# Four column groups for the router logits, and the first mixer chunk moved in between the input turnings

## What is computed

```python
xn = _layernorm(x)
s = _L0_attn_ref(xn, ...)              # the mixer
g = _silu(_L0_ffn_ref(xn, ...))        # mixture of experts, top 1 of 4
x = x + s * g

def _L0_attn_ref(x, ...):
    xn = _rmsnorm(x, rms_w, EPS)
    out_gate = silu(xn @ Wga_w.T) * (xn @ Wgb_w.T)
    f = sigmoid(xn @ Wf_w.T + Wf_b)
    z = (xn @ Wz_w.T) * sigmoid(xn @ Wzg_w.T)
    h = _linear_scan(f, z)             # h[t] = f[t] * h[t-1] + z[t], bfloat16
    return (out_gate * h) @ Wout_w.T + Wout_b + x

def _L0_ffn_ref(x, Wr, br, Wg, Wu, Wd):
    logits = x @ Wr + br               # 4 experts
    top_w, top_idx = top_k(softmax(logits), 1)
    y = (silu(x @ Wg[top_idx]) * (x @ Wu[top_idx])) @ Wd[top_idx]
    return y * top_w
```

## Time and profile before

| | us |
|---|---|
| median of three runs | 1424.99 |
| the profiled execution, its own time | 1422.44 |
| its span, first to last instruction | 1420.6 |
| TensorE busy | 1351.7 (95%) |
| VectorE, ScalarE, GpSimd busy | 1011.4, 880.1, 898.4 |
| mean granted TensorE clock | 0.998 |

### The profile page before, as it was taken

How to read it: one execution, slowest core, us unless ns; L and a number is a source line. 1 busy time by engine, 2 the same in 40 slices (tenths; PEclk the granted TensorE clock), 3 DMA queues, 4 the chain that set the end, 5 groups by cost and what they waited for, 6 DMA issues and landing times.

```text
span 1420.6 us, 24044 instructions
## 1 busy us (share of the span) xinstructions
PE 1351.7 (95%) x8924; PEld 1080.0 (76%) x8924; DVE 1011.4 (71%) x1358; ACT 880.1 (62%) x1459; POOL 898.4 (63%) x570
## 2 busy tenths in 40 slices
PE   7999999999999999998899999999999999999998
PEld 4444559999999988957677777777778678678787
DVE  7755543332232343498998998998989989989897
ACT  3211121111111132488999989999999999999983
POOL 3222211222222212379999998999999999989995
PEclk9999999999999999999999999999999999999999
DMA  9921126766676665331331531523423513513522
GB/s 301 396 97 59 56 84 224 260 260 247 250 268 255 248 226 187 130 88 46 98 93 34 132 92 56 131 68 79 116 75 76 129 50 91 133 46 88 137 68 67
DMA packets 57380, 196.82 MB, mean 139 GB/s; under 512 B 6831, under 2 KB 33583, under 8 KB 49462
## 3 DMA queue, kind: packets, MB, share of 16 engines
q1 hardware_dynamic: 43126, 146.55, 29.3%
q0 software_dynamic: 14144, 48.80, 14.7%
HBM read 141.78 MB, written 31.00 MB: 122 GB/s over the span
## 4 chain that ended last, share of the span: by engine, by line
PE 64%; POOL 17%; ACT 7%; DVE 6%; issue 4%; DMA 1%; SPq 0%; POOLq 0%; DVEq 0%; ACTq 0%
PE bank L1656 17%; POOL hst L733 13%; PE bank L1601 9%; PE bank L1669 9%; PE bank L1830 7%; PE bank L1850 4%; PE bank L1710 4%; ACT dA L940 3%; ACT dbuT L929 3%; DVE hst L1499 3%; PE bank L1702 2%; PE bank L1838 2%; PE bank L1721 2%; PE bank L1740 2%; POOL xpad L676 2%
## 5 line engine op out<-in xcount | busy, mean ns | idle before, releaser
L1499 DVE TENSOR_TENSOR_SCAN hst<-dA,carry,bank 128x512 f32<-128x512 f32 x512 | 632.1, 1269 | 57.3 <-PE bank L1830 37.3
L733 POOL TENSOR_TENSOR hst<-hst,c_bc 128x2048 f32<-128x2048 f32 x127 | 581.8, 4614 | 15.8 <-POOL carry L728 1.8
L940 ACT ACTIVATE dA<-delta,negA 128x512 f32<-128x512 f32 x512 | 353.6, 712 | 7.9 <-DVE hst L1499 7.7
L1830 PEld LDWEIGHTS bank<-ident,dbuT 128*128 128x128 f32 x2048 | 240.1, 141 | 138.5 <-issue 66.4
L1830 PE MATMUL bank<-ident,dbuT 128*128 128x128 f32 x2048 | 311.1, 276 | 32.6 <-DVE hst L1499 28.6
L929 ACT ACTIVATE dbuT<-duT,bT 128x512 f32<-128x512 f32 x382 | 269.0, 711 | 4.9 <-PE bank L1830 4.9
L1656 PEld LDWEIGHTS bank<-f_sb,w_gu 128*128 128x128 f32 x2240 | 256.0, 192 | 4.7 <-issue 2.1
L1656 PE MATMUL bank<-f_sb,w_gu 128*128 128x128 f32 x2240 | 256.9, 275 | 0.7 <-ACT f_sb L797 0.7
L1850 PE MATMUL bank<-ident,hst 128*128 128x128 f32 x1648 | 227.6, 273 | 2.7 <-POOL hst L733 2.4
L661 POOL TENSOR_TENSOR x_sb<-x_sb,neg_half 128x1 f32<-128x1 f32 x35 | 22.6, 647 | 271.4 <-DVE x_sb L1283 271.4
L1850 PEld LDWEIGHTS bank<-ident,hst 128*128 128x128 f32 x1648 | 188.9, 141 | 4.4 <-POOL hst L733 3.9
(11 more groups left out here) (221 smaller groups left out, 1670.1 us busy)
## 6 DMA issues: line engine op xcount, KB each, us to landing
w_gu<-in_w_gu SPq DMA_DIRECT2D x35, 2048.0 KB, 7.5
c_bc<-c_rows SPq DMA_DIRECT2D x64, 512.0 KB, 3.9
hst<-hst POOLq DMA_DIRECT2D x23, 1024.0 KB, 9.0
sorted_x<-sg_a SPq DMA_DIRECT2D x12, 387.0 KB, 11.3
x_sb<-sorted_x SPq DMA_DIRECT2D x35, 129.0 KB, 7.3
x_sb<-in_x SPq DMA_DIRECT2D x8, 512.0 KB, 7.8
w_d<-in_w_d SPq DMA_DIRECT2D x1, 4096.0 KB, 20.3
x_mix<-x_sb SPq DMA_DIRECT2D x1, 4096.0 KB, 30.4
```

The lines of the kernel that those rows point to most:

```text
L733: pool.tensor_tensor(h[:], h[:], c, ALU.mult).then_inc(hc_ready, 1)
L940: act.activation(dA[:, at % DA_BUFS, :], delta[q % B][:, d, :], ACT.Exp, scale=negA[:, d, n:n + 1]).then_inc(dA_ready, 1)
L1499: v.tensor_tensor_scan(h[:, d, :], dA[:, at % DA_BUFS, :], bank[4 + u % 2][:], carry1[q % B][:, n, d:d + 1], ALU.mult, ALU.add).then_inc(s ...
L1830: ins = pe.transpose(bank[4 + u % 2][:, i * P:(i + 1) * P], dbuT[(DS * q + n) % DBU_BUFS][:, i, d * P:(d + 1) * P], ident[:])
```

## The change

1. **Logits.** `w_r` is padded to 32 columns (`QUAD`). Tile i of a chunk is multiplied into partitions 32i to 32i+31 of bank 6, so four matmuls of 128 columns use four column groups of the array. It is done for two chunks at once (16 matmuls for a pair), copied once for the pair, and one matmul with the identity as moving operand (16 columns) brings a chunk's logits to rows.
2. **Order on TensorE.** The turnings use banks 0 and 1 alone. The projections F, ZG, Z, GA and GB of chunk 0, first half, stand between turnings and logits. `ranks` stands in chunk 1.
3. **`w0` on GpSimd.** The scaling moves from ScalarE to GpSimd (`scale_w0`), behind the second of the four `rr0` steps and ahead of the third.
4. **Order on VectorE.** The biases' split, choosing, ranking and placing are spread over chunks 0 and 1: choosing behind the sum of chunk 0, ranking between the halves of chunk 1, placing behind the sum of chunk 1. The rows of chunk 1 get a second buffer (`xn_st_1`, in the second `w_gu` buffer) and a second index tile, and the scatters of chunks 0 and 1 are released together once placing is done. `rows(2)` waits for both chunks' scatters, `rows(3)` for those of chunk 2.
5. **SyncE** stores the mixed rows of chunks 0 and 1 first, then loads `w_gu` for slot 0, waits for the scatters of chunks 0 and 1, then loads slot 1.
6. `mix_st`, `tri`, `ones`, `empty` and `wo_r` move to other buffers.

```diff
-GAP = 152
+GAP = 96
+QUAD = 32
...
-        w_r = sb(l0, "w_r", [P, KB, NE])
+        w_r = sb(l0, "w_r", [P, KB, QUAD])
...
-        mix_st = rt[:].rearrange("p k t e -> p (k t e)").rearrange("p (t d) -> p t d", d=D)
-        tri, ones = (z_sb[:].bitcast(F32)[:, s, 0:P] for s in range(SB))
-        empty = sg_a[:].rearrange("p s c -> p (s c)")[:, 0:FILL * WIDE].rearrange("p (t d) -> p t d", d=WIDE)
+        mix_st = xr_st[:]
+        tri, ones = (w_gu[1][:, 0, 1, s * P:(s + 1) * P] for s in range(SB))
+        empty = w_gu[1][:, 0, 0, 0:FILL * WIDE].rearrange("p (t d) -> p t d", d=WIDE)
...
+        xn_st_1 = w_gu[1][:, 1].rearrange("p k f -> p (k f)")[:, 0:TPC * WIDE].rearrange("p (t d) -> p t d", d=WIDE)
+        logitsT = rt[:, 0:TPC].rearrange("p k t e -> p k (t e)")
+
+        wo_r = w_gu[0][:, 0, 0, 0:SB * D].rearrange("p (s d) -> p s d", s=SB)
         xgT = f_sb[:].bitcast(F32).rearrange("p s c -> p (s c)")[:, 0:KB * P].rearrange("p (k t) -> p k t", k=KB)
...
+            store_mixed(0)
+            store_mixed(1)
             sp.wait_ge(eid_ready, 1)
+            sp.wait_ge(split_ready, 1)
+            sp.wait_ge(zero_filled, 16 * (ROWS // FILL))
             load_up(0)
+            sp.wait_ge(scattered, 2 * 16 * TPC)
             load_up(1)
-            with sp.Fori(0, CHUNKS - 1) as c:
+            with sp.Fori(2, CHUNKS - 1) as c:
                 store_mixed(c)
...
+            def scale_w0():
+                pool.wait_ge(ld_w0, 32)
+                pool.wait_ge(ld_small, 16 * 4)
+                for k in range(KB):
+                    pool.tensor_scalar(w0[:, :, k, :], w0[:, :, k, :], cols0[:, k, 0:1], 1.0, ALU.mult,
+                                       ALU.mult).then_inc(w0_scaled, 1)
+
...
+                if k == 1:
+                    scale_w0()
...
+            def scatter_rows(c, idx, rows):
...
+            scatter_rows(0, idx4, xn_st)
+            scatter_rows(1, idx4_1, xn_st_1)
+            with pool.Fori(2, CHUNKS) as c:
+                scatter_rows(c, idx4, xn_st)
...
+            for c in range(0, CHUNKS, 2):
+                turn_inputs(c)
+                turn_inputs(c + 1)
+                if c == 2:
+                    forget(0, 0)
+                copy_logits(c // 2)
+                if c == 2:
+                    gate_z(0, 0)
+                if c == 4:
+                    gate_a(0, 0)
+            mixer_half(0, 1)
+            mixer_half(1, 0)
             act.wait_ge(shifted, 1)
...
+            mixer_half(0, 0, 0, lambda: split_biases(0))
+            split_biases(1)
+            place_biases()
+            take_logits()
+            mixer_half(0, 1, 0)
+            v.wait_ge(xr_turned, KB * CHUNKS)
+            then(rows(0))
+            add_mix(0)
+            choose()
+            mixer_half(1, 0, 0)
+            rank_rows()
+            mixer_half(1, 1, 0)
+            v.wait_ge(zero_filled, 16 * (ROWS // FILL))
+            then(rows(1, xn_st_1))
+            add_mix(1, xn_st_1)
+            place_rows()
+            tags(0)
+            tags(1, xn_st_1, idx4_1)
+            mixer_half(2, 0, 0)
+            mixer_half(2, 1, 0)
+            then(rows(2))
+            tags(2)
+            add_mix(2)
+            assert [STORED[k] % B for k in range(3)] == [0, 0, 0] and 3 < A_CHUNKS
+
+            def mixer(c, b):
+                rows(c)
+                tags(c)
+                mixer_half(c, 0, b)
+                mixer_half(c, 1, b)
+                add_mix(c)
...
+                    wait_past(pe, xrT_ready, KB * (c - 1) + k + 1)
...
+            def logits(p):
+                pe.wait_ge(xrT_ready, KB * (2 * p + 2))
+                wait_past(pe, logits_copied, p)
+                for c in range(2):
+                    for k in range(KB):
+                        for i in range(TPC):
+                            at = ((2 * p + c) * KB + k) * CH + i * P
+                            ins = pe.matmul(bank[6][i * QUAD:(i + 1) * QUAD, c * P:(c + 1) * P], w_r[:, k, :],
+                                            xT[:, at:at + P], start=(k == 0), stop=(k == KB - 1))
                 ins.then_inc(logits_made, 1)
...
+            def turn_logits(c):
+                pe.wait_ge(logits_copied, c // 2 + 1)
+                at = c * TPC * NE
+                pe.matmul(bank[7][:, at:at + TPC * NE].rearrange("p (i e) -> p i e", e=NE), logitsT[:, c % TPC, :],
+                          ident[:].rearrange("p (i e) -> p i e", e=QUAD)[:, :, 0:NE], start=True,
+                          stop=True).then_inc(logits_ready, 1)
...
+            turn_inputs(0)
+            turn_inputs(1)
+            logits(0)
+            turn_inputs(2)
+            turn_inputs(3)
             pe.wait_ge(w0_scaled, KB)
             project(0, 0, PROJ_F)
-            turn_logits(CHUNKS - 1, (CHUNKS - 1) % 2)
+            logits(1)
+            project(0, 0, PROJ_ZG)
+            turn_inputs(4)
+            turn_inputs(5)
+            project(0, 0, PROJ_Z)
+            logits(2)
+            project(0, 0, PROJ_GA)
+            for c in range(TPC):
+                turn_logits(c)
+            turn_inputs(6)
+            turn_inputs(7)
+            logits(3)
+            for c in range(TPC, CHUNKS):
+                turn_logits(c)
+            project(0, 0, PROJ_GB)
             mixer(0, True)
...
```

More of the change, by code:

```diff
@@ L787, in _ @@
-            act.wait_ge(split_ready, 1)
-            mixer(0)
-            with act.Fori(1, CHUNKS) as c:
-                mixer(c)
+            mixer_half(1, 1)
+            with act.Fori(2, CHUNKS) as c:
+                mixer_half(c, 0)
+                mixer_half(c, 1)
             def turn_in(j):
@@ L1097, in _, with split_biases @@
             two_scaled(3)
[L1099 to L1100 removed]
             biases, taken = bias_f[:, 0:3 * D].rearrange("p (b d) -> p b d", d=D), bias_f[:, 3 * D:]
[L1102 removed]
+            def split_biases(k):
+                if k == 0:
+                    v.wait_ge(ld_small, 16 * 4)
+                    v.wait_ge(set_done, 5)
                 part = bias_b[0:PARTS, :, 0, :]
@@ L1105, in _, with place_biases @@
                 then(v.scalar_tensor_tensor(biases, part, taken[:, k:k + 1], biases, ALU.mult, ALU.add))
-            for half in range(2):
-                v.tensor_copy(bias_b[0:PARTS, :, half, :], biases).then_inc(bias_ready, 1)
+            def place_biases():
+                for half in range(2):
+                    v.tensor_copy(bias_b[0:PARTS, :, half, :], biases).then_inc(bias_ready, 1)
             rms = tmp0[:, 2, :]
-            then(v.tensor_tensor(rms, tmp0[:, 1, :], rr0[:], ALU.mult))
-            v.wait_ge(rstd_ready, 1)
-            then(v.tensor_tensor(rms, rms, rstd0[:], ALU.mult))
             def per_tile(x):
@@ new lines, in rank_rows @@
+            def rank_rows():
+                v.wait_ge(exp_ready, 1)
+                then(v.tensor_reduce(rs[:, 2, :], ex, AX_X, ALU.add))
+                then(v.reciprocal(top_w[:], rs[:, 2, :]))
+                v.wait_ge(ranks_ready, 1)
+                then(v.tensor_copy(tot, bank[0][:, 2 * TILES * NE:3 * TILES * NE]))
+                then(v.memset(rs[:, 3, :], 1.0))
+                for e in range(NE):
+                    then(v.tensor_tensor_scan(cum[:, :, e], rs[:, 3, :], tot[:, :, e], 0.0, ALU.mult, ALU.add))
@@ L1195, in rows @@
+                v.wait_ge(v_l0, w5)
+                v.tensor_tensor(gated[:, s, :], og_sb[:, s, :], h_sb[:, s, :], ALU.mult).then_inc(gated_ready, 1)
+                assert k[0] == L0_SB
+            def rows(c, st=xn_st):
+                if st is xn_st:
                     wait_past(v, scattered, 64 * c)
                     wait_past(v, mix_added, 2 * c)
-                    for i in range(TPC):
-                        t = c * TPC + i
-                        v.tensor_scalar(xn_st[:, i, 0:D], x_sb[:, bass.ds(t, 1), :], mean0[:, bass.ds(t, 1)],
-                                        rstd0[:, bass.ds(t, 1)], ALU.subtract, ALU.mult)
```

220 lines of the change are left out of this document (89 added, 131 removed).

## The result

The kernel after takes 1427.93 us (median of 20 runs, 1425.59 to 1431.65); the kernel before, in the same job, 1424.74 us (20 runs, 1422.74 to 1426.79). The ratio is 1.0026, 95% interval 1.0019 to 1.0033: **slower by 3.2 us**. The forecast was 1423.5 us. The time lies inside the range, on the other side of no change. The profiled execution of after took 1431.65 us, the longest of its 20, with a span of 1429.9 us and a granted clock of 0.990 (before: 0.998), so its end must not be read against that of before without care. A difference of 1.3 us at mix(0) between two kernels is therefore within what one front does.

The account below looks back on a forecast made before the run. TensorE, gapless from the mixer on, bounds the kernel; only time ahead of chunk 1 can be won. Lead 10.4 us at mix(1), less 1.9, 4.6, 1.7 and 0.7, leaves 1.5: 1424.99 - 1.5 = 1423.5 us; range 1418.5 to 1428.5.

Parts of the forecast that it names:

- Steps 1 and 2: Front: first projection starts at 24.5 us, behind GpSimd's scaling; TensorE then takes 18.9 us, to 43.4.
- Steps 2 and 3: From the first projection through GB(0,0), ending at 43.4 us, and six projections, 10.3: mix(0) at 53.7, lead 9.2.
- the clock rival: The clock falls at TensorE's gaps in the front, costing another 1.7 us: 1425.2 us; chance 0.10.
- step 2: TensorE from the first projection to the end of GB(0,0): 18.9 us, with logit pairs at 0.85 each.
- Step 5: Chunk 2: VectorE places ahead of the first half, so TensorE waits 1.9 us for og_sb; lead 8.5.
- Step 6: Chunk 3: rows(3) waits for chunk 2's scatters ahead of the first half; TensorE waits 4.6 us; lead 3.9.
- P: The time when chunk 2's projections start, mix(1) + 3.05 us, from which times in chunks 2 and 3 are counted.
- Step 7: Chunk 3: the granted clock falls behind TensorE's wait and costs 1.7 us; lead 2.2.
- Step 8: SyncE's second 2 MB load runs beside chunk 2's scatters and costs 0.7 us, between 0 and 5.4; lead 1.5.
- My rival for this: Chunk 2's scatters queue behind the w_gu load, landing in 8.0 instead of 2.6 us: 1428.2 us; chance 0.11.

Follow-up runs that it names:

- the first of experiment 4: The kernel after with nine unread matmuls in TensorE's gaps ahead of the turnings of chunks 2 and 3: 1426.20 us, ratio 1.0015 to before.
- the first of experiment 6: The kernel after with chunk 3's and 4's rows late, expert numbering later, w0 scaled on ScalarE and 12 unread matmuls: 1416.30 us, ratio 0.9958.
- the last of experiment 7: The first of experiment 6 with both w_gu loads behind chunk 3's scatters: 1414.11 us, ratio 0.9942 to the kernel before.
- Experiment 5: The kernel before with only the tiled logits in place of the serial ones, in the old order: 1425.29 us, ratio 1.0008.
- experiment 1: The kernel after with SyncE's second w_gu load held until chunk 3's scatters have landed: 1422.32 us, ratio 0.9989 to before.
- experiment 3: The kernel after with VectorE making chunk 3's rows behind its two halves and chunk 4's between its halves: 1417.20 us, ratio 0.9947.
- experiment 2: The kernel after with slot 0's 2 MB of w_gu loaded a second time behind slot 1's: 1431.07 us, ratio 1.0047 to before.
- the second of experiment 4: The kernel after with w0 scaled by ScalarE, behind the turning of chunk 2, instead of GpSimd: 1427.35 us, ratio 1.0026 to before.

## Why the prediction was wrong

- **Steps 1 and 2, the start of the first projection.** 24.5 forecast, 24.83 measured, and right by accident. The scaling itself took 3.05 us (forecast 3.5) and was over at 22.87. What the first projection then waited for was the turning at 23.07, late since VectorE's tiles were held for 1.95 us by the scaling (shown: they take 1.39 without it), and 0.9 us longer at the low clock. I had put 0.6 us on the sharing, on GpSimd's side. The rule of the Trainium skill that I quoted, from "SBUF — State Buffer" ("shared port pair"), speaks of exactly this hold, and the trace agrees.
- **Steps 2 and 3, mix(0).** 53.7 forecast, 56.33 measured: 2.6 us. The failed assumption is that the clock stays up in the front. From the start of the first projection to mix(0) it took 31.5 us where the steps say 29.2. The first projection at the low clock is 1.74 of the difference (3.56 us to the next matmul, 1.82 for the same later), just what the clock rival (chance 0.10) priced at 1.7; the 0.9 us on the turning ahead of it lie in the late start above. The other 0.6 is an error of the sum: three kernels with a full clock from there on (the first of experiment 4, the first of experiment 6, the last of experiment 7) need 29.75 to 29.85 us. The next matmul starts 1.0 us behind a logit pair, not 0.85, and a projection between other work takes 1.82 us, not 1.72. That experiment 7 has mix(0) at 53.50, near the forecast, is luck: its first projection starts at 23.65. What brought the fall stands in the rival, but not in the sum of step 2, which counted the logits' saving as time won: the first logits are done at 17.6 us, and then TensorE waits for VectorE's rows, with one set of turnings (1.09 us) until 23.07. Experiment 5 shows that the cheap logits alone can bring the fall.
- **Step 5, chunk 2.** 1.9 forecast, 1.54 measured, cut to 0.32 by moving what VectorE does there: the mechanism is right.
- **Step 6, the order of `rows(3)`.** 4.6 forecast; 4.38 measured where no load runs beside (experiment 1), and gone with `rows(3)` moved (experiment 3): right in mechanism and size (its own terms, P + 36.9 and P + 32.4, give 4.5).
- **Step 7, the clock behind it.** 1.7 forecast; 8.86 - 7.13 = 1.73 in after, 1.49 in experiment 1, 1.80 in experiment 2. Right here, but not a constant: the first kernel of experiment 4 has 2.90 behind much the same wait. Experiment 3 has neither wait nor low clock.
- **Step 8, `w_gu`. This step decided.** I argued that the load is nearly over when the last scatter starts and took 0.7 between 0 and 5.4. The landing was late by 3.5 us against experiment 1 (6.5 and 3.0), the wait by 3.57, and twice the load made the landing later by 3.2 again. The load was issued at 103.2 us, and its like take 7.5 us; the scatters start from 104.97 to 108.77, so load and scatters were under way together (DMA share 1.01 and 1.07 in the windows from 106 to 110 us). My rival for this was to decide "from a landing of 7.0 us on" and was priced at 1428.2; the landing was 6.5 us. With the clock in the front, the other half of the miss, the time came to 1427.93. I had priced the two rivals one by one and gave no chance to both at once, which is what came. Without the load the change is no longer slower: 0.9989 (experiment 1). With the first projection at full clock it is at 1.0015 (experiment 4, first part), not clearly below the 1.0026 of after.
- **In sum** at the first expert matmul: forecast 1.5 ahead; less 2.6 for the front, less 2.65 for the wait of chunk 3 (7.95 against 4.6 and 0.7), plus 0.35 for chunk 2: 3.4 late. The last 0.5 is in no step: a chunk with a wait takes 0.26 us more than the sum of 20.22, its wait and the clock's cost, as mix(1) to mix(2) (22.03 with a wait of 1.54) and mix(2) to mix(3) (30.16 with 7.95 and 1.73) show. That makes 3.9; measured 3.95.

**Open.** In the profiled executions the second layer of after takes 5.3 us longer than that of before, 799.6 against 794.3 us from the first scan's start to the last's (DVE, columns: ns min/median/max, first and last start):

```profile
L1564 DVE TENSOR_TENSOR_SCAN hst<-dA,carry,bank x512: 1245/1270/1282, 611.3 to 1410.9; 128x512 f32<-128x512 f32 x171
```

The scans are as long as before. The granted clock is lower in stretches there (0.87 instead of 0.96 at 600 to 640 us), and the length differs among kernels whose second layer is the same: 794.8 us in experiment 1, 799.6 in the second of experiment 4, 795.9 in the last. The medians don't show so much. I have no run that tells the cause; that the same takes experiment 5's lead in its executions with a lower mean clock is a guess. Open too is why one front starts mix(0) anywhere between 55.05 and 56.33 us.

## What to carry to other kernels

When a transfer's landing stands on the path, ask what else the DMA engines carry between its issue and its landing, and release bulk loads behind it rather than at the same event. When work is taken off TensorE, its gaps grow: list them, and put the price of a fallen clock into the sum, not only among the rivals, where a gap as long as one that stood before a fall in a trace (here 2.2 us) comes ahead of work on the path. Read the same code in several profiles before a difference of 1 us between two kernels is called an effect. And a wait for a slow transfer belongs behind the work that another engine needs, not ahead of it: here this order alone was worth 9.9 us in chunk 3 (after against experiment 3), more than the 7.8 us that the change had won by mix(1).
